# Attention: one of eight units of maxima goes through ScalarE and GpSimd, values two key tiles late, six probability buffers

## The reference

```
qkv = einsum('btf', layernorm(x), w_qkv)      # q, k, v: 4 x 2048 x 16 x 16
scores = einsum('bihd,bjhd->bhij', q, k) * DIM_HEAD ** -0.5
weights = softmax(scores)                     # over j, 2048 wide
attn = einsum('bhij,bjhd->bhid', weights, v)
x = x + attn.reshape(...) @ w_out.T
```

## Time and profile before

| | |
|---|---|
| median of three runs | 3976.86 us |
| the profiled execution's own time | 3977.46 us |
| its span in the trace | 3975.7 us |
| attention stage, from about 794 to 3387 us | 2593 us |
| PE busy over the span | 3748.1 us, 94% |
| DVE busy | 3660.9 us, 92% |
| ACT busy | 2759.7 us, 69% |
| POOL busy | 553.8 us, 14% |
| granted TensorE clock, mean | 0.996 |

### The profile page before, as it was taken

How to read it: one execution, slowest core, us unless ns; L and a number is a source line. 1 busy time by engine, 2 the same in 40 slices (tenths; PEclk the granted TensorE clock), 3 DMA queues, 4 the chain that set the end, 5 groups by cost and what they waited for, 6 DMA issues and landing times. The chain is left out here.

```text
span 3975.7 us, 60671 instructions
## 1 busy us (share of the span) xinstructions
PE 3748.1 (94%) x21885; PEld 1479.4 (37%) x21885; DVE 3660.9 (92%) x6466; ACT 2759.7 (69%) x3175; POOL 553.8 (14%) x816
## 2 busy tenths in 40 slices
PE   5999999999999999999999999999999999999999
PEld 4777765422222222222222222222222222677776
DVE  8999974599999999999999999999999996798887
ACT  3444444388888888888888888888888888244443
POOL 2334330000000000000000000000000000143333
PEclk8999999999999999999999999999999999999999
DMA  3000002210110010001001001001000100100000
GB/s 152 1 1 4 1 10 87 80 33 20 29 31 28 21 36 24 22 28 31 29 20 40 21 26 34 22 27 31 29 20 29 31 28 10 42 17 17 17 17 22
DMA packets 71779, 116.27 MB, mean 29 GB/s; under 512 B 29304, under 2 KB 50744, under 8 KB 69560
## 3 DMA queue, kind: packets, MB, share of 16 engines
q1 hardware_dynamic: 71480, 112.40, 9.8%
HBM read 73.99 MB, written 28.58 MB: 26 GB/s over the span
## 5 line engine op out<-in xcount | busy, mean ns | idle before, releaser
L1336 DVE TENSOR_REDUCE stats<-ps_b 128x1 f32<-128x512 f32 x4016 | 2491.1, 682 | 6.3 <-PE ps_b L1386 4.3
L1323 ACT ACTIVATE probs<-ps_s,exp_scale 128x1024 f32<-128x1024 f32 x2048 | 2170.2, 1111 | 398.3 <-PE ps_s L1422 398.3
L1386 PE MATMUL ps_b<-w_ffn 48*128 48x512 f16 x4016 | 1275.9, 384 | 165.4 <-DVE stats L1336 37.3
L1398 PE MATMUL ps_o<-probs,w_qkvT 128*32 128x512 f32 x8192 | 1091.9, 605 | 0.7 <-ACT probs L1323 0.7
L1422 PE MATMUL ps_s<-w_ffn 51*128 51x512 f16 x4096 | 1082.6, 379 | 2.4 <-ACT probs L1323 2.2
L1386 PEld LDWEIGHTS ps_b<-w_ffn 48*128 48x128 f16 x4016 | 301.0, 93 | 1541.3 <-DVE stats L1336 1403.9
L880 PE MATMUL ps_gu_f<-w_ffn,zT_f 128*128 128x352 f32 x2048 | 630.7, 461 | 1.3 <-DVE x_res L1535 0.9
L880 PEld LDWEIGHTS ps_gu_f<-w_ffn,zT_f 128*128 128x128 f32 x2048 | 380.7, 191 | 192.9 <-issue 4.0
L1422 PEld LDWEIGHTS ps_s<-w_ffn 51*128 51x128 f16 x4096 | 301.0, 93 | 252.9 <-ACT probs L1323 243.2
L696 ACT ACTIVATE silu_f<-ps_gu_f 128x352 f32<-128x352 f32 x256 | 118.3, 463 | 278.5 <-PE ps_gu_f L880 272.7
L944 POOL TENSOR_TENSOR w_ffn<-w_ffn 128x16 f32<-128x16 f32 x64 | 14.2, 221 | 1923.3 <-DVE w_ffn L1342 1725.4
(11 more groups left out here) (164 smaller groups left out, 2422.5 us busy)
## 6 DMA issues: line engine op xcount, KB each, us to landing
w_ffn<-qk_parts_dram SPq DMA_DIRECT2D x256, 128.0 KB
w_ffn<-qk_parts_dram SPq DMA_DIRECT2D x256, 64.0 KB
qk_parts_dram<-factor SPq DMA_DIRECT2D x32, 256.0 KB, 2.5
qk_parts_dram<-first_group SPq DMA_DIRECT2D x32, 256.0 KB, 2.5
factor<-denom_dram SPq DMA_DIRECT2D x64, 128.0 KB, 5.1
out<-x_res SPq DMA_DIRECT2D x16, 512.0 KB, 2.6
v_then_heads<-y SPq DMA_DIRECT2D x224, 32.0 KB
x_res<-in_L_attn_x SPq DMA_DIRECT2D x3, 2048.0 KB, 18.6
```

The source lines that it names most:

```text
L1323: nc.scalar.activation(probs[:, (2 * kt + half) % 4, :], ps_s[:, half, :], ACT.Exp, scale=m.exp_scale[:, g % H:g % H + 1]).then_inc(exped, 1)
L1336: nc.vector.tensor_reduce(mx[:, s, k // 4, bass.ds(k % 4, 1)], ps_b[:, bank, :], AX.X, ALU.max).then_inc(bank_free, 1)
L1386: last = nc.tensor.matmul(ps_b[j:j + STRIP, bank, :], Q[s][M, qt * P + j:qt * P + j + STRIP], K[s][M, kb * 512:(kb + 1) * 512], start=True ...
L1398: last = nc.tensor.matmul(ps_o[32 * c:32 * c + 32, :], V[s][:, kt, :], probs[:, (2 * kt + c // 2) % 4, (c % 2) * 512:(c % 2 + 1) * 512], s ...
```

## The change

1. The key tiles go in pairs. TensorE's order is one string per pair: S a score matmul, M a unit, E a unit that goes the other way, V a value block. The first pair of a head has its own string.
2. One of eight units, E, is not reduced from its bank by VectorE. ScalarE copies it (128x512) to SBUF, between the first and the second exponential of the pair. GpSimd takes halves against each other, 512 to 256 to 128 columns, each step as max(a - b, 0) + b: six operations. VectorE reduces the 128 columns left, behind the third unit of the next pair. The ring still has three banks; a unit waits for the reduction or for the copy, whichever freed its bank (`bank_reduced`, `bank_evicted`).
3. The value block of a tile comes two tiles late (`LAG`), and there are six probability buffers (`PROBS`).
4. The scale of the exponential comes from a register of ScalarE, loaded once per head index at the stage's start.
5. The head's maximum is placed in pair 6 behind its third unit and the evicted reduction, the transpose in the same pair behind its seventh unit; GpSimd splits ahead of that pair's tree. `keep_o` stands between the third and fourth exponential of a head's first pair. The scaling of results is cut into four parts, one in each of pairs 1 to 4.

The core of the diff:

```
-        nc.scalar.activation(probs[:, (2 * kt + half) % 4, :], ps_s[:, half, :], ACT.Exp,
-                             scale=m.exp_scale[:, g % H:g % H + 1]).then_inc(exped, 1)
+        nc.scalar.activation(probs[:, (2 * at + j % 2) % PROBS, :], ps_s[:, j % 2, :], ACT.Exp,
+                             scale=head_scale[g % H]).then_inc(exped, 1)
...
-    ORDER = ((True, 0), (False, 0), (True, 1), (False, 1), (False, 2), (True, 2), (False, 3), (True, 3))
+    PROBS = 6
+    LAG = 2
+    NEG_AT, TURN_AT = (6, 2), (6, 6)
+    KEEP_AT = 3
+    EVICT_AT = 1
+    EVICTED = 2
+    HALVINGS = (256, 128)
+    REDUCE_AT = 2
+    FIRST_ORDER = "SMSMVEMSSMMSMSVSMS"
+    ORDER = "SMSMVMSESMSSMMVMSS"
...
+                def evict(n, e):
+                    act.wait_ge(bank_full, n + 1)
+                    if e >= EVICTED:
+                        act.wait_ge(evicted_reduced, e - EVICTED + 1)
+                    nc.scalar.copy(evictions[e % EVICTED], ps_b[:, n % RING, :]).then_inc(bank_evicted, 1)
...
+                def tree(e):
+                    at = evictions[e % EVICTED]
+                    pool.wait_ge(bank_evicted, e + 1)
+                    for n, width in enumerate(HALVINGS):
+                        one, other = at[:, 0:width], at[:, width:2 * width]
+                        step = e * TREE_STEPS + 3 * n
+                        nc.gpsimd.tensor_tensor(one, one, other, ALU.subtract).then_inc(tree_step, 1)
+                        pool.wait_ge(tree_step, step + 1)
+                        nc.gpsimd.tensor_scalar(one, one, 0.0, None, ALU.max).then_inc(tree_step, 1)
+                        pool.wait_ge(tree_step, step + 2)
+                        nc.gpsimd.tensor_tensor(one, one, other, ALU.add).then_inc(tree_step, 1)
...
+                for g in range(NH):
+                    for p in range(PAIRS_OF_TILES):
+                        if p == NEG_AT[0] and g + 1 < NH:
+                            pool.wait_ge(neg_step, (g + 1) * NEG_STEPS)
+                            minus_max(g + 1)
+                        trees(g, p)
...
+                    if n >= RING:
+                        place, evicted = order_of_units[n - RING]
+                        pe.wait_ge(bank_evicted if evicted else bank_reduced, place + 1)
```

More of the change, by code:

```diff
@@ L1211, in attend_phase, with units_before @@
         o_kept = m.o_kept
[L1213 to L1243, removed]
+        def units_before(head, evicted):
+            return sum(1 for row in plan for _, _, h, _, _, e in row if h <= head and e == evicted)
         with nc.Block() as block:
@@ L1301, in _, with trees @@
+                def trees(g, p):
+                    for _, _, _, _, e, evicted in units_of(g, p):
+                        if evicted:
+                            tree(e)
                 for s in range(SLOTS):
@@ L1367, in _ @@
-                heads(dve, body, lambda: None)
+                for g in range(NH):
+                    for p in range(PAIRS_OF_TILES):
+                        if p == INVERT_AT and g >= 1 and g % GROUP == 0:
+                            invert_denominators(nc, dve, m, g // GROUP - 1)
+                        here = {i: unit_at for i, *unit_at in units_of(g, p)}
+                        for i in range(8):
+                            if i in here:
+                                n, head, k, _, evicted = here[i]
+                                if not evicted:
+                                    unit(n, head, k)
+                            if i == REDUCE_AT and (g, p) > (0, 0):
+                                reduce_evicted(*((g, p - 1) if p > 0 else (g - 1, PAIRS_OF_TILES - 1)))
+                            if (p, i) == NEG_AT and g + 1 < NH:
+                                minus_max(g + 1)
+                            if (p, i) == TURN_AT and g + 1 < NH:
+                                turn_neg(g + 1)
@@ L1369, in _, with unit @@
             @block.tensor
             def _(pe):
[L1371 to L1382 removed]
+                def unit(n, head, k):
+                    s = head % 2
+                    if k == (LEAD if head == 1 else 0):
+                        pe.wait_ge(max_loaded[s], HEAD_LOADS * (head // 2 + 1))
+                    if n >= RING:
+                        place, evicted = order_of_units[n - RING]
+                        pe.wait_ge(bank_evicted if evicted else bank_reduced, place + 1)
@@ L1432, in tail @@
-                def tail():
-                    values(NH - 1, (NH - 1) % SLOTS, KT - 1)
-                heads(pe, body, tail)
+                for g in range(NH):
+                    for p in range(PAIRS_OF_TILES):
+                        here = {i: unit_at for i, *unit_at in units_of(g, p)}
+                        scores = units = products = 0
+                        for token in order_of(p):
+                            if token == "S":
+                                score(g, 2 * p + scores // 4, scores % 4)
+                                scores += 1
+                            elif token in "ME":
+                                if units in here:
+                                    n, head, k, _, _ = here[units]
+                                    unit(n, head, k)
+                                units += 1
+                            else:
+                                at = g * KT + 2 * p - LAG + products
+                                if at >= 0:
+                                    values(at)
+                                products += 1
@@ L1438 @@
+                for at in range(NH * KT - LAG, NH * KT):
+                    values(at)
 class Merge:
```

220 lines of the change are left out of this document (107 added, 113 removed).

## The result

The changed kernel takes 4042.11 us (median of 4 runs, 4041.04 to 4042.71) against 3976.85: 65 us slower, ratio 1.0162 with a 95% interval of 1.015 to 1.0174. The forecast was 3931, faster, in a range of 3840 to 4035. The sign was wrong, and the time lies outside the range.

The account below looks back on a forecast made before the run. The prediction took VectorE, ring and value block together to bound the attention stage. Heads -44 us, after the last transpose -1.8, last head -3, register loads and extra values +3, total -46 from 3976.9: 3931 us, range 3840 to 4035.

Parts of the forecast that it names:

- The pair: Steady pair of tiles in the attention stage: 4.74 us instead of 4.98, set by the loop through the third exponential.
- the copy row: Profile row of a 1024-column ScalarE copy without scale operand, 1.013 us; taken as the register-scaled exponential's price, 1.01 against 1.111.
- The first rival: Pair gets no shorter: the register costs what the operand did, pair 4.94, total 4008 us; chance 0.27.
- The wait at the head's end: TensorE waits some 2.0 us per head for the DMAs' rows, ready 6.6 us after the transpose starts.
- The rival without a wait: At the head boundary the rows land by 9.48, in 4.6 us: head 37.90, total 3808 us; chance 0.11.
- its 1.70: At the head boundary, time from a small DMA's last issue to its waiter's start, 1.70 us, read from the trace.
- The late tree: Rival: GpSimd's chain exceeds 4.5 us instead of 3.25 and VectorE waits; +130 to some +500 us; chance 0.12.
- the head's sum: One head: first pair 4.68, five pairs of 4.74, last two pairs 11.45; 39.87 us with 0.04 for inversion, against 40.58.
- its first pair, 4.68: A head's first pair, with its own order: 4.68 us by TensorE's own chain, the third exponential ending at 4.39 to 4.5.
- the three rivals: Pair no shorter (0.27), no wait at the head boundary (0.11), late GpSimd tree (0.12).
- The last head: Last head, without units: shorter exponentials take four in about 3.96 instead of 4.34 us over eight pairs, -3 us.
- The start: Sixteen register loads before the stage's first exponential, plus one tile more of values at the end: +3 us (0 to 10).

Follow-up runs that it names:

- e7: Changed kernel with unit lead 24 instead of 16 and no unit evicted, VectorE reducing all eight: 3997.08 us, ratio 1.0046.
- e4: Changed kernel with the exponential's scale as a 128x1 memory operand again, no register loads: 4056.89 us, ratio 1.0193.
- e1: Changed kernel with units 24 instead of 16 ahead, head maximum and transpose in pair 5, row DMAs a pair more: 3934.8 us, ratio 0.9899.
- e5: Changed kernel (lead 16) with no evicted unit in pair 6, where GpSimd splits the head's maxima: 4040.51 us, ratio 1.0162.
- e6: Changed kernel with lead 24 and no evicted unit in pair 5, where the maxima are split: 3912.42 us, ratio 0.9837.
- e2: Changed kernel with seven overwritten score-shaped matmuls on TensorE at each head's start but the first, while it waits for the rows: 3987.14 us, ratio 1.0003.
- e8: Kernel before, with only the transpose two key tiles later (tile 14 instead of 12): 4242.84 us, ratio 1.0666.
- e9: e6 with the denominators' inversion moved to pair 4 and GpSimd's four scalings to pair 5 of two heads: 3870.07 us, ratio 0.973.
- e3: Changed kernel with seven overwritten score-shaped matmuls filling TensorE's wait before the last head only: 4026.37 us.
- e11: Changed kernel with an unread unit-shaped matmul (48x512) in the last head wherever the order has a unit: 4015.99 us, ratio 1.0095.
- e10: e9 with the sixteen register loads moved to the end of ScalarE's work in the stage before: 3868.50 us, ratio 0.9726.

## Why the prediction was wrong

*The pair.* Right: 4.74 forecast, 4.67 measured. The register saves what the copy row promised (1.026 for 1.01), and e7 and e4 show both parts earn (0.38 and 0.16). The first rival is out.

*The wait at the head's end.* Right in its cause and nearly in its size: the transpose starts 4.91 into pair 6 (4.85 forecast), the first score 6.48 behind it in the median (6.6), and from the first exponential of pair 6 to the next head's it is 11.33 in the mean (11.45). TensorE itself stands still for less than the 2.0 of the forecast, 0.93 in the median, since pair 7 is longer than assumed. The rival without a wait is out, and e1 shows it from the other side. The prediction also set the fixed part of about 2.0 us that the Trainium skill gives (DMA: Bandwidth & Descriptors, Anatomy of one DMA) against its 1.70. That section is on DMAs that GpSimd issues, and these are issued by SP; the changed kernel shows 1.70 again.

*The late tree.* This rival is half right. The chain is 4.16 us, not 3.25: the estimate took one-input steps at the price of a copy and 0.11 us of each as fixed, which no row shows, and the one-input step of 256 columns took 0.843 for 0.40. With the split before it the chain is 1.4 late once a head, not in every pair. By e5 the DMAs still set the next head's first score without it. By e6 against e1 it costs about 1.5 us a head once the wait for the DMAs is gone, of which 0.96 is the price of leaving it out.

*The step that failed* is a term of the head's sum, 4.68 + 5 x 4.74 + 11.45: **its first pair, 4.68, was priced at full clock and by TensorE's chain alone, though it stands behind a new wait of TensorE.** In the mean of the 62 heads that pair is 6.18, five pairs are 23.61 (23.70) and the last two 11.33 (11.45). So this one term is 1.50 short, and the head 1.25. Of the 1.50, 1.0 is the half clock (5.18 at full clock against 6.18), and 0.50 stands at full clock too, where ScalarE sets the pair and not TensorE. e2 holds the clock up and wins 48 us over 62 heads; e8 brings the half clock about in the kernel before. None of the three rivals had the clock either. The trace before showed a granted clock of 1.00 through the stage. The Trainium skill (TensorE: Matmul & The Clock Gate, What's actually happening) does say that the array's clock depends on how busy the engine has been of late, and is throttled otherwise; the runs agree, with 0.50 behind the wait and 1.00 where the wait is filled (e2) or gone (e9). I had read the clock as full and priced a new wait of TensorE as if it stayed so.

With the clock held up (e2) most heads are 39.85, the forecast's 39.87. That is luck in part: the 0.5 missing in the first pair is offset by pairs of 4.67 instead of 4.74 and by a slightly shorter head's end.

*The last head* was to give 3 us and took 23 more. e3 shows that this is the clock: with the same work at full clock it takes 33.0, 0.9 less than before. TensorE is busy for all 20 us of the changed kernel's row, and at 1.2 GHz. With units beside the scores (e11) the clock comes back, without them it stays down for 57 us.

*The start.* "+3 (0 to 10)" for the register loads: the first exponential came 4.9 us later (800.0 against 795.1), and the first head maximum 7.9. The other 3 us fall in the stage's start at half clock, 17 us of it against 3; that these are cause and effect was not tested.

The difference of forecast and result, term by term: heads (41.12 - 39.87) x 62 = 77.5 us; behind the last head maximum +23.7 instead of -1.8 - 3, 28.5; before the first 7.9 instead of 3, 4.9. Together 111, which is 4042 - 3931.

What beats both kernels is e10, 3868.5: the pair of the change, with the DMAs given a pair of tiles more, GpSimd relieved in the pair where it splits the maxima, and the rare steps put where there is room.

## What to carry to other kernels

When a change brings a wait of TensorE into a stage that had none, price the wait and the work behind it at both clocks, and look in each stretch at the granted clock beside the busy share, since a full share at half clock looks like work. When a stage's period gets shorter, every fixed time in it (a DMA's way, a split on another engine) needs more of the shorter steps to hide: move its start first. An engine that goes from 5% busy to near the length of the period, as GpSimd did here (a chain of 4.16 in a pair of 4.67), has no room left for its rare steps. And sum every engine's chain in each special stretch, such as a head's first pair, not only in the steady one.

## What the runs showed of the hardware that was not expected

- In the last head of the changed kernel TensorE stayed at half clock for 57 us though the profile shows it busy throughout: tiles of 3.68 us. The same head, entered at full clock (e3), kept full clock with the same work, tiles of 2.08. With one 48x512 matmul more per score matmul (e11) it came back to 2.4 GHz within the first pair and took 34.4 us.
- Short pauses were enough for the clock to fall: in the changed kernel TensorE stood about 0.9 us before a head's first score, with another pause shortly before, and 48 of 62 heads began at half clock.
- GpSimd's one-input step against an immediate is dearer than its two-input step of the same 256 columns: 0.843 against 0.726 us. A copy of 256 columns took 0.396 in the earlier trace rows.
- An exponential with its scale in a register took 1.026 us, with a 128x1 operand 1.111 to 1.118. Sixteen register loads from SBUF delayed the first exponential by 3.6 to 5.0 us (798.6 to 800.0 in the runs of lead 16 that have them, 795.0 in e4).
